# Idle products moved: seven products of ones in TensorE's wait for the root's tables, fourteen instead of twenty-two ahead of the last norm's transposes

## The reference

```
x = x + cross_attention(layernorm(x), ctx, ctx)      # 16 heads of 32, then a 512x512 projection
x = x + gated_scan(layernorm(x))                     # rms norm, in-projection, scan over 128 tokens, out-projection
x = x + mixture(layernorm(x))                        # 2 shared and 8 routed experts, top 2, width 512
```

## Time and profile before

| what | value |
|---|---|
| time, median of 3 runs | 521.34 us (521.06 to 521.61) |
| time of the profiled execution | 521.11 us |
| its span in the profile | 519.3 us |
| mean granted clock of PE | 0.974 of full speed |
| busy: PE / DVE / ACT / POOL | 483.9 / 403.6 / 332.4 / 274.8 us |
| idle products of ones (L1173) | 52 records, 7.7 to 26.9 us |
| idle products of identity (L1275) | 44 records, 311.4 to 317.1 us |

### The profile page before, as it was taken

One profiled execution on the slowest core, in us unless ns is written; L12 is line 12 of the kernel. 1 busy time (PEld: TensorE's weight loads), 2 busy tenths in 40 slices (PEclk: granted clock), 3 DMA queues, 4 the chain that ended last, 5 costly groups with the idle time before them and its releaser, 6 DMA issues.

```text
span 519.3 us, 16078 instructions
## 1 busy us (share of the span) xinstructions
PE 483.9 (93%) x6871; PEld 343.7 (66%) x6871; DVE 403.6 (78%) x611; ACT 332.4 (64%) x371; POOL 274.8 (53%) x262
## 2 busy tenths in 40 slices
PE   4999879889999999999989999998999999999994
PEld 4456656566766676776766559645787878787642
DVE  3757867678877788878758787787899999989426
ACT  3356677567767668766575267464788988878310
POOL 0438887998999999999960213461010111100051
PEclk9759989999999999999999999999999999999998
DMA  6998957899897988889989220278999999997144
GB/s 225 245 290 229 248 155 230 237 269 251 208 272 247 265 261 259 221 223 319 328 314 359 74 82 2 66 258 326 394 366 416 418 419 418 416 414 290 40 122 142
DMA packets 29822, 133.99 MB, mean 258 GB/s; under 512 B 6452, under 2 KB 6708, under 8 KB 18996
## 3 DMA queue, kind: packets, MB, share of 16 engines
q1 hardware_dynamic: 26072, 120.91, 71.6%
q0 software_dynamic: 3680, 12.06, 6.4%
HBM read 96.77 MB, written 11.01 MB: 208 GB/s over the span
## 4 chain that ended last, share of the span: by engine, by line
PE 54%; DVE 29%; issue 8%; DMA 4%; POOL 2%; ACT 2%; SPq 0%; DVEq 0%; ACTq 0%; POOLq 0%
DVE ws L832 10%; PE bank L1096 9%; PE bank L1156 9%; DVE mx L766 8%; PE bank L1141 7%; PE bank L1165 6%; DMA wst<-in_ffw 3%; PE bank L1231 3%; PE bank L1309 2%; PE bank L1307 2%; PE bank L1308 2%; POOL ps L682 2%; PE bank L1173 2%; DVE hf L1012 2%; DVE hl L1017 2%
## 5 line engine op out<-in xcount | busy, mean ns | idle before, releaser
L766 DVE TENSOR_REDUCE mx<-bank 128x1 f32<-128x512 f32 x240 | 154.9, 686 | 53.9 <-PE bank L1096 52.0
L508 ACT ACTIVATE pt<-bank 128x1024 f32<-128x1024 f32 x128 | 124.4, 1023 | 56.9 <-PE bank L1141 50.6
L682 POOL TENSOR_TENSOR ps<-pt 128x512 f32<-128x512 f32 x120 | 149.6, 1272 | 1.0 <-ACT pt L508 0.5
L832 DVE SCALAR_TENSOR_TENSOR ws<-wst,ws 128x2048 f16<-128x2048 f32 x51 | 116.7, 2309 | 2.6 <-ACT ws L564 2.5
L564 ACT ACTIVATE ws<-wst 128x2048 f16<-128x2048 f32 x48 | 90.5, 1904 | 5.0 <-DMA wst<-in_ffw 4.7
L1322 PE MATMUL bank<-xt,ws 128*128 128x128 f16 x480 | 81.2, 219 | 0.8 <-DVE hf L1012 0.8
L1324 PE MATMUL bank<-xt,ws 128*128 128x128 f16 x480 | 81.2, 219 | 0.0
L1323 PE MATMUL bank<-xt,ws 128*128 128x128 f16 x480 | 81.2, 219 | 0.0
L723 POOL DMA_DIRECT2D ys_rows<-xn x15 | 8.1, 543 | 121.4 <-ACT xn L639 121.4
L658 POOL TENSOR_TENSOR kl<-kt,kh 128x512 f16<-128x512 f32 x58 | 67.3, 1182 | 9.1 <-ACT kh L454 6.8
L1156 PE MATMUL bank<-pt,v 128*32 128x128 f32 x2048 | 70.0, 276 | 2.2 <-issue 2.2
(11 more groups left out here) (190 smaller groups left out, 763.5 us busy)
## 6 DMA issues: line engine op xcount, KB each, us to landing
wst<-in_ffw SPq DMA_DIRECT2D x51, 1024.0 KB, 10.8
kt<-in_keysT SPq DMA_DIRECT2D x16, 1024.0 KB, 6.2
v<-in_vals SPq DMA_DIRECT2D x16, 1024.0 KB, 9.1
kstk<-kh SPq DMA_DIRECT2D x88, 128.0 KB, 4.7
kstk<-kl SPq DMA_DIRECT2D x44, 128.0 KB, 3.2
wst<-kh SPq DMA_DIRECT2D x40, 128.0 KB, 4.7
xs_rows<-biases SPq DMA_DIRECT2D x15, 256.0 KB, 7.7
x_tok<-xs_rows POOLq DMA_DIRECT2D x15, 256.0 KB, 8.8
```

The costliest lines, as they stand in the source:

```text
L508: act.activation(pt[:, n % 4, :, :, :].rearrange("p j a t -> p (j a t)"), bank[:, 2 * (n % 2):2 * (n % 2) + 2, :].rearrange("p j n -> p (j ...
L682: pool.tensor_tensor(ps2[:, n % 4, :, :], pt[:, n % 4, 0, :, :], pt[:, n % 4, 1, :, :], ALU.add)\
L766: dve.tensor_reduce(mx[:, a, q:q + 1], bank[:, 4 + k % 2, :], AX.X, ALU.max).then_inc(m_taken, 1)
L832: dve.scalar_tensor_tensor(ws[:, home_of(q), 1, m, :, :].rearrange("p c n -> p (c n)"), wst[:, q % 2, m, :, :].rearrange("p c n -> p (c n) ...
```

## The change

Two edits. `keep_busy` gets a parameter for the bank that it writes. In the third group, ahead of `scores(18)`, PE now waits until the bank that the next maximum will use is taken, and issues seven products of ones into it. Ahead of the transposes of the last norm 6, 3 and 5 idle products stand in place of 10, 6 and 6.

```diff
@@ -1168,9 +1168,9 @@
 
         pe.wait_ge(ones_set, 1)
         pe.wait_ge(id_in, 16)
-        def keep_busy(count):
+        def keep_busy(count, n=7):
             for _ in range(count):
-                pe.matmul(bank[:, 7, 0:P], one[:, :], one[:, :], start=True, stop=True)
+                pe.matmul(bank[:, n, 0:P], one[:, :], one[:, :], start=True, stop=True)
 
         pe.wait_ge(one_set, 1)
         keep_busy(20)
@@ -1187,6 +1187,10 @@
                     max_scores(j, k)
                 if p == 1 and a == 1 and i + 2 < G:
                     queries(i + 2)
+                if i == 2 and p == 0 and a == 0:
+                    j, k = tenants[1]
+                    pe.wait_ge(m_taken, MB * j + k - 1)
+                    keep_busy(7, 4 + k % 2)
                 scores(n)
             for j, k in tenants[2:]:
                 max_scores(j, k)
@@ -1341,7 +1345,7 @@
         FIRST, SECOND = slice(0, T // 2), slice(T // 2, T)
         for b in range(B):
             if b < 3:
-                idle_products(3, (10, 6, 6)[b])
+                idle_products(3, (6, 3, 5)[b])
             transpose_tokens(b)
         pe.wait_ge(w_lo[0], 1)
         pe.wait_ge(w_lo[1], 1)
```

## The result

The changed kernel takes 523.61 us in the median of 22 runs, against 521.49 us for 22 runs of the kernel before beside it: a ratio of 1.0047, 95% interval 1.0025 to 1.0070. It is slower by some 2.1 to 2.4 us. The forecast was 522.3 us, up to 522.9. The sign of its likeliest case was right (it gave most of the weight to "same", though), its size was less than half.

What follows compares the result with a forecast made beforehand. The prediction took POOL's chain to bound the third group's transposes, making the low clock there free. Moved clock fall +1.55 and norm -0.57 gave +0.98 us on a 521.34 us median: 522.3 us, range 520.4 to 522.9.

Steps and rivals of the forecast that it cites:

- likeliest case: Third group and norm: the clock's fall moves behind the transposes and the norm gains; 522.3 us, chance 0.50.
- What bounds the third group: Transposes of queries at 75.51 us wait for POOL's chain, so the low clock from 69.5 us costs nothing.
- A's products: Third group: seven products take 1.57 us in PE's first idle stretch, scores 0.14 us late, at no cost.
- The moved fall: Behind the transposes at 75.51 us: after 2.43 us idle the clock falls for 3.4 us, costing 1.55 us.
- It passes on: Keys 5 to the values' products at 107.17 us: a PE delay before 86 us delays this chain equally.
- the sum: Whole kernel: +1.55 for the moved fall, -0.57 for the norm, +0.98 us in all.
- B: Last norm: eight fewer idle products bring the last transposes earlier, -0.57 us, with DVE the next one late.
- The transposes' rule: Rival, last norm: transposes do not hold the clock, it falls near 318 us, costing 1.55 us; chance 0.06.
- The low stretch is 6.8 us long: Rival, behind the transposes of queries: the slow stretch lasts twice as long, +3.1 us, 523.9 us; chance 0.06.

Runs made afterwards that it cites:

- The norm alone: Only the fewer idle products ahead of the last norm's transposes (6, 3, 5), against the kernel before: 521.31 us, ratio 1.0006.
- POOL's half first: Only POOL's low half of the queries moved ahead of pair sums 16 and 17, against the kernel before: 521.65 us, ratio 0.9994.
- the ones alone: Only the seven products of ones in the third group, norm as before, against the kernel before: 523.85 us, ratio 1.0043.
- the ones with 13 at the start: Seven products of ones in the third group, 13 instead of 20 at the start, norm as before, against the kernel before: 521.89 us, ratio 1.0008.
- change with 13: The whole change with 13 products of ones at the start in place of 20, against the kernel before: 521.32 us, ratio 0.9998.
- the pure shifts: Only seven or fourteen more products of ones at the very start (28 or 56 instructions), against the kernel before: 522.63 us, 1.0010; 521.28 us, 0.9986.
- the kernel with ten more products: The seven products plus ten ahead of the transposes of queries, norm as before, against the kernel before: 525.11 us, ratio 1.0064.
- the four wide products: Two products of 512 columns in each idle stretch of the third group, norm as before, against the kernel before: 522.31 us, ratio 1.0021.
- the better version: Two wide products in the first stretch, POOL's half first, norm 6, 3, 5, 18 products at the start, against the kernel before: 518.96 us, 0.9945.

## Why the prediction was right or wrong

**What bounds the third group: right.** The transposes stand 8.1 us behind exponential 16 in nine of the ten executions with POOL's old order (8.34 in the tenth, where ten products stood ahead of them), whether the clock was low, high or falling. With POOL's order changed they moved to 5.7, 5.7 and 6.9 in three kernels of four (8.17 in the fourth, whose ones ran at the low clock). So the low clock at 69.5 was free. The norm alone had 6.8 us of it from 68.2 on and still took 17.42 us from 16 to 24; with POOL's half first, where no slack is left, the low clock costs: 6.93 us to the transposes, 5.68 without it.

**A's products: right.** 14 records, 1.66 us to the scores behind them (1.57 forecast), no cost at their own place. From the first scores to the last maximum 4.07 us (4.08 forecast), then 2.58 us of wait (2.43).

**The moved fall: right, with its size.** Three executions show it (the change, the ones alone, the ones with 13 at the start), at 19.03, 19.04 and 19.01 us against 17.42: 1.6 us, against 1.55 in the sum. It takes an execution in which keys 4 come in time. Where PE had already waited over 3 us for them, the clock was low before the products came and no second fall followed. How often that is, no run shows, and the timed runs don't confirm the 1.6 us by themselves: the ones with 13 products at the start, one of the three, are +0.4 us in time. From exponential 16 to 40 the three take 52.4 to 53.3 us, the other seven with POOL's old order 49.7 to 52.0, the kernel before the longest of these; so the fall is still seen at 40.

**"It passes on": right as far as 110 us.** The values' products waited for their load as before (109.21 against 107.17 in the earlier trace rows): it was issued at 99.74 in place of 97.47 and landed 9.4 us later in place of 9.6, each time 0.1 us before them. But "no load there that is tied to an earlier place" was too strong. In the execution of the norm alone exponential 24 comes 2.10 us late and exponential 40 0.09 us late; in that of the ones alone 1.22 becomes 0.18, with the load issued 0.68 us late, at 98.15, and landing after 8.9 us, at the same 107.1. The stretch from 24 to 40 took 32.3 to 34.6 us. A delay is passed on in some executions and swallowed in others.

**The term that failed: the products' instructions.** I costed the seven products as 14 records of 0.112 us at their own place, and the sum, +1.55 - 0.57, has no term for what they do to the program behind them. There PE's program is 28 instructions longer. Record 1737 then falls into a row of value products, and PE stalls there. All four executions with a shift of 28 have it (0.89, 0.88, 1.17, 0.33 us), none of the ten others. From exponential 40 to 127 those four take 158.85 to 160.07 us, 159.34 in the mean; the five with no shift there (before, norm alone, 13 at the start, POOL's half first, change with 13) 157.56 to 157.73, 157.66 in the mean. In the change's own execution it is 1.1 us, in the mean of the four 1.7, and it stood in no term and no rival. The other five take 157.66 to 158.47; the three of them above 158 have shorter breaks, 0.10 to 0.24 us, at records 1610, 2622 and 2623. The change's own execution adds up to 1.6 + 1.1 - 0.6 = 2.1 us, and its span is 2.35 us longer; the rest is 0.4 us by a load of keys ahead of the edit, and small steps either way. With the mean of the four it would be 2.7 us, against 2.1 to 2.4 measured.

How far the timed runs bear this out: the ones alone against the ones with the length kept (1.0043 and 1.0008), and the change likewise (1.0047 and 0.9998), point the same way. The second pair's intervals overlap by 0.0003, the first pair's by more. In both pairs the start differs too, so they are not a clean proof; the pure shifts (1.0010 and 0.9986) differ in the right direction, with intervals that overlap. What is shown is the stall, its place, the packet of instructions ahead of it, and its dependence on the shift in the traces; how much of the 2.1 to 2.4 us of time it makes in the median is not.

**B: right.** 0.61 us where 0.57 was forecast, by DVE as the next one late (last transposes after 0.59 us of wait for it).

**The rivals.** The transposes' rule did not decide: with 14 products in place of 22 the clock was 1.00 from 312 to 320 us. "The low stretch is 6.8 us long" did not come about behind the transposes; it was 3.4 us each time. It was 6.8 us in three executions in which PE had waited 1.6 us or more ahead of it for keys. The range ended at 522.9 because it held only the clock's terms.

**What stays open.** Why the kernel with ten more products takes 525.1 us in the median while its one profile shows 519.2 us, and why the four wide products cost 1.1 us in the median and nothing in theirs. Filling the second stretch would cost where that stretch isn't idle, as in the executions in which PE comes late to it; this was not tested. Nor is it shown why the better version gains 2.7 us, when its marks give 1.4 (16 to 24) + 0.6 (norm) = 2.0, and when the same two steps in the attention, without the norm's and with 8 instructions more, gave nothing (1.0003).

## What to carry to other kernels

Before you warm an engine in a wait, look at the next wait on its path: if another engine sets that one, the clock's fall moves there, and behind it the work may have no slack. Here the only version that gained shortens the second wait at its source (POOL's order) and fills only the first; with the norm's edit and the length kept it was timed only as a whole, and POOL's order alone, and with two wide products, didn't show in the time. Count the instructions you add, not only their time: in a long unrolled program everything behind them is shifted, and a 1 us stall can come or go 60 us later, so compare a variant with one of the same program length. Two wide products fill the same wait with 8 instructions in place of 28.

## What the runs showed of the hardware that I had not expected

- PE can stall for 0.3 to 1.2 us in the middle of a row of equal products, with no semaphore that the profile shows, at fixed counts of its records (1483, 1737, 3509, 4525 of some 6,870, multiples of some 127 apart), 1.29 to 1.58 us behind the end of a 16 KB packet of instructions. 28 more instructions at the very start brought two such stalls, 56 none of those two but one of 0.24 us at record 1610.
- The same kernel's executions differ by several us (the change: 520.1 to 528.1; before beside it: 518.4 to 527.2), and part of it is made before 63 us: in the profiled executions the wait for keys 4 ahead of the third group lasted from nothing to 3.5 us. It was 1.1 to 3.5 us in four of the five whose start had been faster (exponential 12 before 55.1 us), where the load took 10.9 us or more, and nothing in the fifth (the ones with 13 at the start), where it took 7.8. One profile each shows the mechanism, not the size of a difference below 1%.
- Idle runs of PE that a fall of the clock followed behind 40 us lasted 1.69 us (before), 2.04 and 2.58 (ones alone, the change), 2.59 (ones, 13 at the start) and 1.64 to 3.51 in the other kernels. The one of 1.40 us in the earlier trace rows was followed by none, nor was one of 1.73 us at 469.7 in the profile of POOL's half first alone: length alone doesn't decide it.
